# Linear attention beside pair-sorted experts on one core: the second biases move from the visits into the attention's output bank

## What is computed

```python
xn = layernorm(x)
# attention, heads of 8
Q, K, V = xn @ Wq, xn @ Wk, xn @ Wv
Qf, Kf = elu(Q) + 1, elu(K) + 1
num = Qf @ (Kf.T @ V);  den = Qf @ sum(Kf) + 1e-6
att = (num / den) @ Wo
# experts: probs = softmax(xn @ gate_w.T + gate_b), the best two of 8
h = relu(xn @ w1[e] + b1[e])
ffn = sum over the best two e of probs[e] * (h @ w2[e] + b2[e])
out = x + att + ffn
```

## Time and profile before

| | us |
|---|---|
| median of 3 runs | 120.92 |
| lowest and highest run | 119.16, 121.91 |
| the profiled execution | 118.78 |
| its span, first to last instruction | 117.0 |

### The profile page before, as it was taken

How to read it: one execution, slowest core, us unless ns; L and a number is a source line. 1 busy time by engine, 2 the same in 40 slices (tenths; PEclk the granted TensorE clock), 3 DMA queues, 4 the chain that set the end, 5 groups by cost and what they waited for, 6 DMA issues and landing times.

```text
span 117.0 us, 3091 instructions
## 1 busy us (share of the span) xinstructions
PE 101.4 (87%) x771; PEld 90.5 (77%) x771; DVE 68.6 (59%) x287; ACT 60.5 (52%) x171; POOL 51.0 (44%) x66
## 2 busy tenths in 40 slices
PE   6947989999797899989899999999999999999100
PEld 6946867667676777679899999999999999989000
DVE  0858988997719945011565556647567566574600
ACT  0657996444020221549466677776677667755000
POOL 5005800467777778011000403114505557887870
PEclk9999999999999999999999999999999999999955
DMA  3998000001111114999944665757577768962522
GB/s 93 279 339 365 11 0 6 0 24 48 54 63 57 48 55 128 250 252 346 311 110 127 131 165 145 174 136 171 162 162 161 185 154 165 198 112 23 45 22 25
DMA packets 16656, 15.52 MB, mean 133 GB/s; under 512 B 1920, under 2 KB 16256, under 8 KB 16512
## 3 DMA queue, kind: packets, MB, share of 16 engines
q1 hardware_dynamic: 13248, 12.88, 37.8%
q0 software_dynamic: 2816, 2.18, 12.9%
q10 hardware_dynamic: 576, 0.27, 0.8%
HBM read 12.09 MB, written 3.23 MB: 131 GB/s over the span
## 4 chain that ended last, share of the span: by engine, by line
issue 28%; PE 24%; POOL 19%; DVE 11%; DMA 10%; ACT 2%; POOLq 2%; SPq 1%; DVEq 0%
POOL out L459 19%; DMA x_tok<-in_x 5%; DMA out<-res 4%; PE banks L970 4%; PE banks L1031 3%; PE banks L1036 3%; PE banks L939 3%; PE banks L992 3%; PE banks L1007 2%; POOLq L115 2%; DVE att L777 1%; PE banks L923 1%; DVE idx L645 1%; PE banks L1018 1%; PE banks L969 1%
## 5 line engine op out<-in xcount | busy, mean ns | idle before, releaser
L552 ACT ACTIVATE h<-banks,w_now 128x128 f32<-128x128 f32 x118 | 36.9, 365 | 17.7 <-PE banks L1067 17.7
L459 POOL DMA_INDIRECT out<-acc,token x16 | 25.1, 1570 | 33.7 <-DVE acc L801 32.4
L1067 PE MATMUL banks<-xsT,w_now 128*128 x236 | 36.5, 278 | 0.7 <-DMA w_now<-in_w1b 0.4
L1080 PE MATMUL banks<-w_all,h 128*128 x236 | 36.1, 277 | 0.0
L1067 PEld LDWEIGHTS banks<-xsT,w_now 128*128 128x128 f32 x236 | 30.9, 192 | 1.4 <-issue 1.2
L1080 PEld LDWEIGHTS banks<-w_all,h 128*128 128x128 f32 x236 | 31.0, 192 | 0.3 <-issue 0.2
L793 DVE TENSOR_TENSOR y<-banks,w_all 128x128 f32<-128x128 f32 x59 | 17.2, 292 | 22.4 <-PE banks L1080 13.5
L801 DVE SCALAR_TENSOR_TENSOR acc<-y,xs,acc 128x128 f32 x59 | 20.7, 352 | 1.1 <-DVE y L793 0.9
L444 POOL DMA_INDIRECT sorted_dram<-xrow,slot x16 | 15.9, 991 | 5.3 <-issue 4.6
L895 PE MATMUL banks<-ones 128*128 128x128 f32 x42 | 7.4, 337 | 1.1 <-POOL ones L387 1.1
L895 PEld LDWEIGHTS banks<-ones 128*128 128x128 f32 x42 | 7.0, 250 | 1.5 <-POOL ones L387 1.1
(11 more groups left out here) (99 smaller groups left out, 115.4 us busy)
## 6 DMA issues: line engine op xcount, KB each, us to landing
w_now<-in_w1b SPq DMA_DIRECT2D x59, 129.0 KB, 2.7
w_all<-in_w SPq DMA_DIRECT2D x1, 1536.0 KB, 9.2
out<-res SPq DMA_DIRECT2D x4, 256.0 KB, 5.0
xs<-sorted_dram SPq DMA_DIRECT2D x3, 276.0 KB, 4.7
x_tok<-in_x SPq DMA_DIRECT2D x3, 256.0 KB, 6.1
xs<-sorted_dram SPq DMA_DIRECT2D x2, 138.0 KB, 3.3
x_tok<-in_x SPq DMA_DIRECT2D x2, 128.0 KB, 2.5
sorted_dram<-xrow,slot POOLq DMA_INDIRECT x16, 2.3
```

What stands on the lines that cost most here:

```text
L459: nc.gpsimd.indirect_dma_start(out=out_rows, out_offset=bass.IndirectOffsetOnAxis(ap=token[:, s:s + 1], axis=0), in_=acc[:, s * D:(s + 1) ...
L552: nc.scalar.activation(h[:, i % NH, c, :], h_ps[i % NHP][:, c * P:(c + 1) * P], ACT.Relu, bias=w1_now[:, i % NW, H + c:H + c + 1]).then_in ...
L1067: last = nc.tensor.matmul(h_ps[i % NHP][:, c * P:(c + 1) * P], w1_now[:, i % NW, c * P:(c + 1) * P], xsT[:, bass.ds(toff, P)], start=True, ...
L1080: last = nc.tensor.matmul(y_ps[i % NYP], h[:, i % NH, c, :], w2_all[:, bass.ds(woff + c * D, D)], start=(c == 0), stop=(c == KC - 1))
```

## The change

The second biases leave the visits. DVE and POOL keep the eight gate values of every token in `gates` as well; PE turns them (`transpose_gates`: four products into the ranks' bank), ACT copies them to `gatesT` (32 x 512), and `project_out` opens its bank with four products of `gatesT` with `b2_blocks`, a 32 x 512 matrix that holds `b2` once for each of four tiles. The residual, which the identity product brought, is added by DVE where ACT copied the sum (`residual`). In a visit DVE runs `accumulate` alone, straight from the bank, and loads two lists of offsets instead of three. `w2` is stored without `b2`'s 128 columns (1032 KB in place of 1536).

Queries lose their opening product; ACT makes exp and relu from the same bank, and DVE min and add. `wq` and the gate's bias move from ACT's DMA queue to SP's, behind `x` and the constants. Logits are taken four tiles at a time, pairs in groups of 8, 4 and 4 tiles, and the gate values of the first eight tiles in one step each in place of two. The calls are written in another order on DVE, PE and ACT; the table of visits is made earlier.

```diff
             sp.dma_start(cst[:], consts).then_inc(consts_in, 16)
+            sp.dma_start(gate_bias[:], gate_b.partition_broadcast(P)).then_inc(gate_b_in, 16)
+            sp.dma_start(wq_f[:], wq).then_inc(wq_in, 16)
             sp.dma_start(wo_f[:], wo).then_inc(wo_in, 16)
+            sp.dma_start(b2_f[:], b2_blocks).then_inc(b2_in, 16)
             sp.dma_start(w2_all[:], w2).then_inc(w2_in, 16)
...
-            nc.scalar.dma_start(wq_f[:], wq).then_inc(wq_in, 16)
-            nc.scalar.dma_start(gate_bias[:], gate_b.partition_broadcast(P)).then_inc(gate_b_in, 16)
...
             def exp_q(k):
                 act.wait_ge(q_done, k + 1)
-                nc.scalar.activation(qf[:, blk_cols(k)], q_ps[k], ACT.Exp, bias=minus_one[:, 0:1]
-                                     ).then_inc(qexp_done, 1)
+                nc.scalar.activation(qf[:, blk_cols(k)], q_ps[k], ACT.Exp).then_inc(qexp_done, 1)
+                nc.scalar.activation(q_relu[:, blk_cols(k)], q_ps[k], ACT.Relu).then_inc(qexp_done, 1)
...
-            def copy_sum(k):
...
+            def copy_gatesT():
+                act.wait_ge(gatesT_done, 1)
+                nc.scalar.copy(gatesT[:], gatesT_ps).then_inc(gatesT_copied, 1)
...
+            def residual(k):
+                dve.wait_ge(wo_done, k + 1)
+                nc.vector.tensor_tensor(res[:, blk_tiles(k), :], wo_ps[k].rearrange("p (t d) -> p t d", t=4),
+                                        x_tok[:, blk_tiles(k), :], ALU.add).then_inc(res_done, 1)
...
-            def take_y(i, woff):
-
+            def accumulate(i, toff, goff):
                 dve.wait_ge(l2_done, i + 1)
-                if i >= 2:
-                    dve.wait_ge(acc_done, i - 1)
-                nc.vector.tensor_tensor(y[:, i % 2, :], y_ps[i % NYP], w2_all[:, bass.ds(woff + KC * D, D)], ALU.add
-                                        ).then_inc(y_done, 1)
-
-            def accumulate(i, toff, goff):
-                dve.wait_ge(y_done, i + 1)
                 mine = acc[:, bass.ds(toff, D)]
                 if i:
                     dve.wait_ge(acc_done, i)
-                nc.vector.scalar_tensor_tensor(out=mine, in0=y[:, i % 2, :], scalar=xs[:, bass.ds(goff, 1)], in1=mine,
+                nc.vector.scalar_tensor_tensor(out=mine, in0=y_ps[i % NYP], scalar=xs[:, bass.ds(goff, 1)], in1=mine,
                                                op0=ALU.mult, op1=ALU.add).then_inc(acc_done, 1)
...
             def order_visits():
 
                 pe.wait_ge(table_step, 4)
-                pe.wait_ge(kvmask_done, 3)
+                pe.wait_ge(slot_done, 2)
...
+            def transpose_gates():
+                pe.wait_ge(table_done, 1)
+                pe.wait_ge(gates_done, 1)
+                pe.wait_ge(gates_dve_done, 1)
+                for k in range(NBLK):
+                    last = nc.tensor.transpose(gatesT_ps[:, k * P:(k + 1) * P],
+                                               gates[:, blk_tiles(k), :].rearrange("p t e -> p (t e)"), ident_t[:])
+                last.then_inc(gatesT_done, 1)
...
-                nc.tensor.matmul(wo_ps[k].rearrange("p (t d) -> p t d", t=4), ident_t[:], x_tok[:, blk_tiles(k), :],
-                                 start=True, stop=False)
+                for j in range(4):
+                    nc.tensor.matmul(wo_ps[k][:, j * P:(j + 1) * P], gatesT[:, k * P:(k + 1) * P],
+                                     b2_f[:, j * P:(j + 1) * P], start=(j == 0), stop=False)
```

More of the change, by code:

```diff
@@ L324, in normalised, with pairs_known @@
             return [sum(len(n) for n in norm[:i + 1]) for norm in (NORM_DVE, NORM_ACT, NORM_POOL)]
+        def pairs_known(t):
+            return sum(t >= a for a, _ in PAIR_GROUPS)
         def group_of_visit(i):
@@ L889, in _, with warm_up @@
         def _(pe):
-            def warm_up(times, after=0):
+            def warm_up(times, where=warm_ps):
                 pe.wait_ge(ones_set, 1)
-                if after:
-                    pe.wait_ge(slot_done, after)
                 for _ in range(times):
-                    last = nc.tensor.matmul(warm_ps, ones[:], ones[:], start=True, stop=True)
+                    last = nc.tensor.matmul(where, ones[:], ones[:], start=True, stop=True)
                 last.then_inc(pe_warm, 1)
```

302 lines of the change are left out of this document (148 added, 154 removed).

## The result

The changed kernel took 119.88 us in the median of 20 runs (118.50 to 121.71), the kernel before 120.03 us in the median of 20 runs (117.37 to 121.91). The ratio is 1.0101, with a 95% interval of 1.0057 to 1.0145; it leaves out of both kernels the executions that lie over 1.5% above the fastest one, which keeps 13 of the changed kernel's 20 and four of the other's. So the change brought nothing: the medians lie 0.1% apart, and the 1% that it costs by the ratio rests on four runs of the kernel before. Forecast was a gain of 1.1%. The profiled execution took 120.47 us with a span of 118.7 us, where the forecast was 117.5 us with a span of 115.7.

What follows compares the result with a forecast made beforehand. PE alone bounds the middle of the visits, so gains lie at their start, holes and end: 1.3 - 0.75 - 1.86 = -1.3 us, put on the median of 120.92, gives 119.6 us, range 117.3 to 122.2.

Steps and rivals of the forecast that it cites:

- The front: From the loads of x to DVE's pairs' sum: fourth part 0.8 sooner, sum starting at 21.9 instead of 22.45.
- The middle up to the second numerator: DVE and PE steps behind the pairs' sum: PE waits 2.3 us for the table, second numerator at 38.75, 2.3 later.
- The step that failed: Output blocks on PE: four 128-column bias products cost 0.89, the replaced identity product 0.86 to 0.94, so no change.
- the clock, a rival held at 0.13: PE's new waits: clock falls to 1.2 GHz, losing 1.5 to 2 us; 121.3, or 123 if both; chance 0.13.
- The visits: PE's waits for rows and the seventh w1 go, since the table is made earlier: -0.75 us, between 0 and that.
- The tail: Behind PE's last product: last give_back starts 1.65 later instead of 3.51, -1.86 us; POOL paces, DVE done at 0.7.
- The sum: Whole kernel: 1.3 - 0.75 - 1.86 = -1.3 us; profiled span 117.0 to 115.7, median 120.92 to 119.6.
- the 13.5 of the sum: Output blocks: second numerator to last block's end takes 13.5 us, the former 14.48 less 0.52, 0.24 and 0.2.

Runs made afterwards that it cites:

- e3: Kernel before with the loads of wq and the gate's bias moved from ACT's queue to SP's; 118.08 us, ratio 0.991.
- e10: Changed kernel with the loads of wq and the gate's bias back on ACT's queue; 121.27 us, ratio 1.008.
- e8: Changed kernel with the visits' table and the first divide back at their old, later places; 115.89 us, ratio 0.971.
- e12: Changed kernel with the first divide back behind the last finish_q, table still early; 117.75 us, ratio 0.987.
- e1: Changed kernel with products of ones in PE's waits before order_visits and before the second numerator; 118.03 us, ratio 0.987.
- e7: Changed kernel with both PE waits filled by products of ones, and gatesT and second biases in 128 partitions; 116.43 us, ratio 0.976.
- e14: Changed kernel with the first divide back behind the last finish_q, and gatesT and second biases in 128 partitions; 116.24 us, ratio 0.970.
- e5: Changed kernel with ten products of ones in PE's wait before order_visits alone; 117.67 us, ratio 0.983.
- e11: Kernel before with the table made early and the fourth queries moved ahead of the first numerator; 117.70 us, ratio 0.984.
- e4: Kernel before with one DVE step a visit, accumulate reading the bank, second biases left out of the output; 117.68 us, ratio 0.983.
- e2: Changed kernel with gatesT and the second biases held in 128 partitions, 96 of them zero; 118.56 us, ratio 0.992.
- e6: Changed kernel with eight products of ones in PE's wait before the second numerator alone; 118.67 us, ratio 0.990.
- e13: Kernel before with the first divide moved ahead of the last finish_q steps; 120.23 us, ratio 1.001.

## Why the prediction was wrong

**The front: right in effect, its first term too small.** 0.8 was forecast for the fourth part of `x`, and 21.9 for the pairs' sum. The fourth part landed 4.3 us after its issue in place of 6.1, so 1.8 sooner; not all of that passed on. The pairs' sum started at 21.61, 0.84 sooner than before; alone the move gave 1.06 (e3), and its undoing cost 0.89 (e10).

**The middle up to the second numerator: right, step by step.** 38.75 forecast, 38.30 measured; the new wait 2.42 against 2.3, `visited` there at 29.45 against 30.0, the first divide from 34.99 against 35.4. What the sum did not part is what each move costs. By the stretches, both late is 12.27 us behind the pairs' sum (e8), the table early 15.57 (e12), and the divide early on top 16.69. So the change's other edits gained 1.74 there (14.01 to 12.27), and its two moves took 3.30 and 1.12. The divide stood in the sum with its full 1.51 us; that it could have stood 3 steps later, where PE does not wait for it, I did not ask. At the last block the early table costs 1.70 (28.15 us behind the pairs' sum in e8, 29.85 in e12), since its products are then gone from among the blocks, and it gives back part of that in the visits.

**The step that failed: "four products of 128 columns for the biases cost what the four of `wo` cost (0.89) ... no change".** With the `wo` group behind them they cost 0.34 to 0.39 us more a block, 1.45 us for the four (e1 against e7; 1.44 for e12 against e14), through the change from weights of 128 rows to 32 and back. The price came from groups that have full rows.

**The second step that failed: the clock, a rival held at 0.13 and at nothing in the sum.** In the profiled executions a fall in the middle cost 1.66 us of the blocks (15.94 against 14.28, three kernels), as that rival had it (1.5 to 2); its time of 121.3 us did not come in the median. Against it I had set that PE works between the waits; the rows show that this did not help: with the first wait filled, the second one, of 1.9 us, was still enough in the profiled execution of e5. The change also takes out the products of ones that the kernel before has ahead of its second `keys_values` and its second numerator (L895 in the list of PE's products above), just where the two waits open; what that alone does was not tried, but e1 puts such products back and the clock stayed up. The rule of the Trainium skill (TensorE: Matmul & The Clock Gate, section "HAM oscillation — how this bites in real kernels") that products behind a wait start at half rate agrees with the rows behind the second wait (0.51 from 38.8 to 42.2 us) and not with those behind the first, where 2.42 us left the clock at 1.00. That section of the Trainium skill makes it hang on how long the wait is, which the prediction left out.

**The visits: right in size, hidden here.** -0.75 forecast, +0.21 in the profiled execution. In the kernel before, the early table makes the visits 0.91 shorter (e11), and the nine other kernels with an early table took 55.28 to 56.51, the six with a late one (before among them) 56.13 to 57.67. In the profiled execution PE stood 0.56 us at 94 us for a `w1` load that landed late, which the prediction had ruled out; why it was late is not shown.

**The tail: right.** -1.86 forecast, -1.75 measured, and -1.75 alone (e4); DVE was done 0.77 us behind PE's last product (0.7 forecast), and POOL set the rest, as forecast.

**The sum.** The span came out 3.0 us above the forecast's 115.7: rows 1.45, clock 1.66, visits 0.94 (57.77 us from the last block to the last product in place of 56.83), tail 0.11, less the 0.45 of the second numerator and 0.67 by which the blocks, rows and clock taken off, were shorter than the 13.5 of the sum. Those terms close, for one execution of each kernel. They do not close for the medians: the profiled execution of before lies 1.25 us below its median and the changed kernel's 0.59 above, so that the 1.7 us between the two executions is a gain of 0.15 between the medians. What the other executions of the kernel before lost, no trace shows. Without the rows and the fall (e7) the same order of work is 2.4% faster than before. That 119.6 lies near the measured 119.88 is no merit of the sum: it was put on a median of three runs, 120.92, that 20 runs put at 120.03.

Why an early table holds the second numerator back by 3.30 us in the changed kernel and by 0.86 in the kernel before can be read from the timelines. Behind `order_visits` there is no difference: from its start to the second numerator it is 7.68 us in e12 and 7.67 in e11. What differs is that `order_visits` starts 7.89 us behind the pairs' sum in e12 and 7.20 in e11, where DVE has one `finish_k` less on the way (0.65), and what the early table is held against: 12.27 us in e8 and 14.01 in the kernel before, which has the fourth queries between its first two numerators. 0.69 and 1.74 make up the 2.44. What stays open is the fourth queries' move by itself, and how often the clock falls, since each kernel has one trace.

## What to carry to other kernels

When a small product is put between large ones, price the change of its weights' rows at both ends, and pad with zeros where it counts. A step moved ahead on an engine should be weighed against each step that it passes: ask which of them another engine waits for. A gain that opens a wait on PE has to be counted with a fall of the clock behind it, and a few useless products in the wait are a cheap test of that. And when one part of a change is tried alone, list what else its edit moves before its price is read.

## What the runs showed of the hardware

Weights of 32 rows between products of 128 rows: the first two products of the group, and the first two behind it, start 0.20 to 0.22 us after the one ahead in place of 0.11 to 0.12, and the loads there begin only after the loads ahead have ended; padded to 128 rows, the group runs at 0.89 us for eight products like any other. The granted clock fell to 0.5 for about 3.4 us behind PE's waits of 2.4 us (e2) or of 1.9 us (changed, e5, e10), and stayed at 1.00 behind waits of 2.4 us in e6, e12 and e14; it fell in the front too, for up to 6.9 us (e13). A fall cost 1.66 us where it met the output blocks and 0.83 where it came ahead of the second numerator. With both waits filled by products of ones it stayed up (e1, e7).
